# Normalised rows turned by a DMA transpose instead of TensorE, attention rows read from PSUM, and GpSimd's slot in another order

## The chip, the cores and the metric

The kernel runs on one core of a Trainium2 chip. A core has TensorE (PE, with its weight loads listed as PEld), VectorE (DVE), ScalarE (ACT), GpSimd (POOL) and SyncE (SP), which here only issues DMAs. Each engine works through its own list of instructions in order and waits on semaphores. The metric is the device time of one execution in microseconds; lower is better.

## The reference

The input holds 128 graphs of 128 nodes with 256 features each. The first step is a layernorm with ReLU; then come three layers, each an attention over the graph's neighbours and a feed-forward block of width 1024; at the end the input is added back.

```
h = max(layernorm(x), 0)
for l in 0..2:
    si, sj = h @ attn_w[l, :256], h @ attn_w[l, 256:]
    scores = leaky_relu(si[:, :, None] + sj[:, None, :] + attn_b[l], 0.2)
    attn   = softmax(where(adj + eye > 0, scores, -inf))
    n      = layernorm(h + attn @ h) * g1[l] + beta1[l]
    ff     = gelu(n @ W1[l] + b1[l]) @ W2[l] + b2[l]
    h      = layernorm(n + ff) * g2[l] + beta2[l]
return x + h
```

Everything is float32. The kernel computes each large product as three float16 products (high by high, high by low, low by high), where a value's low part is the value less its high part.

## The kernel before

Four graphs (`T` = 4) make one group, and one group in one layer is an item: 32 groups by 3 layers are 96 items. Items run in rings of eight groups: eight groups through layer 0, the same eight through layer 1, then layer 2, then the next eight. The program of every engine is a list of slots, one slot per item, written by hand: slot `s` holds the hidden layer of item `s`, and beside it the steps of neighbouring items: the end of item `s-1` and the attention of items `s+1` and `s+2`. Within a slot the order follows `c`, one of the eight blocks of 128 hidden columns.

TensorE's slot: for each `c` six matmuls of 512 columns for the hidden block (`hidden`, L366), then twelve of 256 columns for the feed-forward output (`feed`, L380), three blocks behind (`LAG` = 3), so that the first three blocks of a slot finish item `s-1`. After `c` = 0 the aggregation of item `s+1` (`aggregate`, L422: twelve matmuls). After `c` = 4 the eight transposes of item `s+1`'s normalised rows (`transpose_norm1`, L432) and the four of `spread_sj` for item `s+2` (L404), which spread a column of scores over the partitions. In `c` = 7 the four transposes of item `s+2`'s attention probabilities (`transpose_probs`, L410).

The normalised rows of item `s+1` are made like this. VectorE adds the aggregation to the rows (`attention_residual`, L650), takes their statistics (L579) and, after `hidden` of `c` = 0 in the next slot, aggregates them (L584 to L587). GpSimd raises the variance to the power -1/2 (L786) and forms the shift (L788). ScalarE applies both (`norm_attention`, L488, writing `norm1`). TensorE turns `norm1` into a PSUM bank pair (L432), ScalarE copies that to float16 `hT_hi` (`high_hT`, L534) and VectorE subtracts to get `hT_lo` (`split_hT`, L665). Both are needed by the first hidden block of the next slot: the first four matmuls read `hT_hi`, the last two `hT_lo`.

GpSimd's slot: `inverse_deviation` for item `s+1` (L786, L788); `h_residual`, two operations of 1024 elements (L798, L800), which waits until VectorE has made the dot products of item `s+2`; `low_X` (L804); then for item `s-1` `inverse_deviation`, `norm_feed` (L812, four operations) and, at the slot's end, `layer_output` (L826, L828, each twice). In slots whose item `s-2` is in layer 2 there is also `skip_connection` (L835), and in slots that start a group's layer 0 one more `inverse_deviation`.

VectorE's slot starts with the dot products of item `s+2` at `c` = 1 (L613 and L616, four of each, both reading `X` and `attn_rows` from SBUF). Of each hidden block, ScalarE makes the gelu (L478) and its float16 copy `g_hi` (L483), and VectorE the low part `g_lo` (L572); three PSUM banks hold hidden blocks (`PF_RING`), one bank the attention rows (`p_att`) and two pairs of banks (`p_pair`) the rest.

In the slots in which a new ring of groups comes in (eight of every 24, called heavy slots below; the others are light), VectorE takes the statistics of a group's input and makes its mask, and ScalarE makes the input's norm (`norm_input`, L488, four operations after `c` = 7).

All DMAs are issued by SP, in order, on one queue: group inputs `x_in` and `adj_in`, weights, stores and a second load of `x` for the last addition.

## Time and profile before

| | |
|---|---|
| median of three runs | 2402.95 us (2402.5 to 2403.74) |
| the profiled execution | 2401.22 us, span 2399.4 us |
| TensorE busy | 2333.0 us (97%) |
| ScalarE busy | 1892.0 us |
| VectorE busy | 1869.7 us |
| GpSimd busy | 1698.2 us |
| granted TensorE clock | 9 tenths or more in 39 of the page's 40 slices |
| DMA | 70.83 MB, 30 GB/s on average |

The profiled execution's span is what the trace covers; its own time is 1.8 us more. A matmul's duration in the trace is that of its whole passage through a pipelined array, so successive matmuls overlap, and the distance between their starts is what each costs.

### The profile page before, as it was taken

Reading aid. Unit: us, or ns where it says so; the run is one execution under the profiler, and the core shown is the slowest. Engines: PE = TensorE matmul, PEld = TensorE weight load, DVE = VectorE, ACT = ScalarE, POOL = GpSimd, SP = SyncE. Lnnn points to the kernel's source line nnn. Section 1 sums busy time; section 2 is a strip of 40 time slices with the busy share of each in tenths; the row PEclk is TensorE's granted clock in tenths of the full one; section 3 lists DMA queues with packets and bytes.
Section 4 is the critical chain, followed back from the end, with each engine's and each line's share of the span. In section 5 each row is a group of like instructions: output and inputs, shape, how many; then the busy total and the mean of one; then the engine's idle time right before and its main releaser. Section 6 shows DMA issues by size and latency. Waiting matters only on the chain.

```text
span 2399.4 us, 47629 instructions
## 1 busy us (share of the span) xinstructions
PE 2333.0 (97%) x16608; PEld 1649.3 (69%) x16608; DVE 1869.7 (78%) x5974; ACT 1892.0 (79%) x3498; POOL 1698.2 (71%) x1543
## 2 busy tenths in 40 slices
PE   3999999999999999999999999999999999999997
PEld 2667777776666777777666777777766677777775
DVE  6887777777888777777888787878788877787874
ACT  4878787878888878787888877778788887878783
POOL 3567676768887666667887767676878776767686
PEclk9999999999999999999999999999999999999998
DMA  5200000001211000001121000000121100000012
GB/s 162 87 28 27 1 1 2 1 19 41 93 62 36 1 1 1 1 1 36 54 78 60 23 2 1 1 1 2 53 67 63 41 2 1 1 1 1 19 42 65
DMA packets 77421, 70.83 MB, mean 30 GB/s; under 512 B 7040, under 2 KB 75648, under 8 KB 77184
## 3 DMA queue, kind: packets, MB, share of 16 engines
q1 hardware_dynamic: 77184, 67.79, 9.1%
q8 instruction: 134, 2.20, 0.4%
q14 instruction: 103, 0.84, 0.1%
HBM read 51.01 MB, written 16.78 MB: 28 GB/s over the span
## 4 chain that ended last, share of the span: by engine, by line
PE 66%; POOL 16%; DVE 11%; ACT 3%; issue 2%; POOLq 0%; DVEq 0%
PE p_pair L380 29%; PE p_hid L366 28%; PE p_pair L422 4%; PE p_pair L432 2%; POOL rstd L786 2%; DVE dots L613 2%; DVE g_lo L572 2%; POOL w_f L835 2%; POOL h_res L798 2%; POOL h_res L800 2%; POOL norm L812 2%; DVE res L675 2%; POOL w_f L828 2%; POOL X_lo L804 2%; POOL w_f L826 2%
## 5 line engine op out<-in xcount | busy, mean ns | idle before, releaser
L380 PE MATMUL p_pair<-w_hi,g_hi 128*128 128x256 f16 x3072 | 837.6, 273 | 0.0
L380 PE MATMUL p_pair<-w_lo,g_hi 128*128 128x256 f16 x3072 | 837.6, 273 | 0.0
L380 PE MATMUL p_pair<-w_hi,g_lo 128*128 128x256 f16 x3072 | 837.5, 273 | 0.0
L572 DVE TENSOR_TENSOR g_lo<-p_hid,g_hi 128x512 f16<-128x512 f32 x768 | 528.6, 688 | 396.2 <-ACT g_hi L483 389.7
L478 ACT ACTIVATE p_hid<-p_hid,b_eff 128x512 f32<-128x512 f32 x768 | 504.5, 657 | 316.9 <-PE p_hid L366 315.7
L798 POOL TENSOR_TENSOR h_res<-norm,g_rows 128x1024 f32<-128x1024 f32 x96 | 227.7, 2372 | 384.0 <-DVE res L675 377.3
L483 ACT ACTIVATE g_hi<-p_hid 128x512 f16<-128x512 f32 x768 | 458.6, 597 | 24.4
L366 PE MATMUL p_hid<-hT_hi,w_hi 128*128 128x512 f16 x1536 | 458.2, 380 | 1.5 <-DVE g_lo L572 1.4
L366 PE MATMUL p_hid<-hT_hi,w_lo 128*128 128x512 f16 x1536 | 458.3, 380 | 0.0
L366 PE MATMUL p_hid<-hT_lo,w_hi 128*128 128x512 f16 x1536 | 457.9, 380 | 0.0
L786 POOL TENSOR_TENSOR rstd<-var_eps,minus_half 128x4 f32<-128x4 f32 x224 | 242.2, 1081 | 259.0 <-DVE minus_mean L587 253.7
L380 PEld LDWEIGHTS p_pair<-w_lo,g_hi 128*128 128x128 f16 x3072 | 300.7, 98 | 106.5 <-issue 0.3
L380 PEld LDWEIGHTS p_pair<-w_hi,g_hi 128*128 128x128 f16 x3072 | 300.7, 98 | 105.6 <-issue 0.4
L380 PEld LDWEIGHTS p_pair<-w_hi,g_lo 128*128 128x128 f16 x3072 | 300.7, 98 | 34.8
L488 ACT ACTIVATE norm<-res,shift,rstd 128x256 f32<-128x256 f32 x384 | 199.4, 590 | 97.6 <-POOL shift L788 97.6
L366 PEld LDWEIGHTS p_hid<-hT_hi,w_lo 128*128 128x128 f16 x1536 | 150.6, 98 | 182.2 <-issue 1.7
L366 PEld LDWEIGHTS p_hid<-hT_lo,w_hi 128*128 128x128 f16 x1536 | 150.6, 98 | 182.2 <-issue 1.7
L579 DVE BATCH_NORM_STATS2 bn<-res 128x6 f32<-128x256 f32 x768 | 269.5, 416 | 3.3
L800 POOL TENSOR_TENSOR h_res<-h_res,res_rows 128x1024 f32<-128x1024 f32 x96 | 227.0, 2364 | 7.5
L812 POOL TENSOR_SCALAR norm<-res,rstd,shift 128x256 f32<-128x256 f32 x384 | 207.5, 555 | 10.0
L650 DVE SCALAR_TENSOR_TENSOR res<-p_pair,row_inv,X 128x256 f32<-128x256 f32 x384 | 159.1, 477 | 67.6 <-PE p_pair L422 67.5
L804 POOL TENSOR_TENSOR X_lo<-X,X_hi 128x1024 f16<-128x1024 f32 x96 | 204.6, 2132 | 0.0
(68 smaller groups left out, 3658.5 us busy)
## 6 DMA issues: line engine op xcount, KB each, us to landing
x_in<-in_x SPq DMA_DIRECT2D x32, 512.0 KB, 4.1
w_f<-in_x SPq DMA_DIRECT2D x32, 512.0 KB, 5.8
out<-w_f SPq DMA_DIRECT2D x32, 512.0 KB, 4.2
adj_in<-in_adj SPq DMA_DIRECT2D x32, 256.0 KB, 4.5
w_f<-in_L_gnn_W SPq DMA_DIRECT2D x6, 1024.0 KB, 6.1
attn_rows<-in_L_gnn_attn_w SPq DMA_DIRECT2D x1, 768.0 KB, 5.9
g_rows<-in_L_gnn_g SPq DMA_DIRECT2D x2, 384.0 KB, 7.5
b_rows<-in_L_gnn_b SPq DMA_DIRECT2D x1, 384.0 KB, 6.7
```

The costliest lines, as they stand in the source:

```text
L366: mm = pe.matmul(p_hid[in_ring(s, c, PF_RING)][:], w[l][:, k, cols], h[i][:, k, :], start=(n == 0), stop=(n == 3 * KD - 1))
L380: mm = pe.matmul(ff_banks(s)[:, t, :], g[i][:, nodes], w[l][:, c, :], start=(c == 0 and t % 2 == 0 and n == 0), stop=(c == C - 1 and n == ...
L478: act.activation(p_hid[k][:], p_hid[k][:], ACT.Gelu, bias=b1_eff[:, l, c:c + 1], scale=1.0 / WSCALE).then_inc(gelu_ready, 1)
L483: act.activation(g_hi[i][:], p_hid[k][:], ACT.Copy).then_inc(g_hi_ready, 1)
L488: act.activation(dst[:, t, :], src[:, t, :], func, bias=shift[n][s % 2][:, t:t + 1], scale=rstd[n][s % 2][:, t:t + 1]).then_inc(done, 1)
L572: dve.tensor_tensor(g_lo[i][:], p_hid[k][:], g_hi[i][:], ALU.subtract).then_inc(g_lo_ready, 1)
L579: dve.bn_stats(bn[n][:, t, :], src[:, t, :]).then_inc(stat_steps[n], 1)
L786: pool.tensor_tensor(rstd[n][s % 2][:], var_eps[n][:], minus_half[:], ALU.pow).then_inc(rstd_ready[n], 1)
L798: pool.tensor_tensor(h_res[i][:], norm1[:], rows(g1_rows, l, T), ALU.mult).then_inc(h_res_steps, 1)
L800: pool.tensor_tensor(h_res[i][:], h_res[i][:], rows(res_rows, l, T), ALU.add).then_inc(h_res_steps, 1)
L804: pool.tensor_tensor(X_lo[:], X[s % RING][:], X_hi[:], ALU.subtract).then_inc(X_lo_ready, 1)
L812: pool.tensor_scalar(norm2[:, t, :], res2[:, t, :], rstd[2][s % 2][:, t:t + 1], shift[2][s % 2][:, t:t + 1], ALU.mult, ALU.add).then_inc(n ...
```

## The change

1. `transpose_norm1`, `high_hT` and `split_hT` are gone. ScalarE copies `norm1` from SBUF to float16 `h_hi` (`high_h`, at `c` = 3), GpSimd subtracts to get `h_lo` (`low_h`), and SP issues one DMA transpose for each of the two (`turn_h`), 128x1024 float16 from SBUF to SBUF, into `hT_hi` and `hT_lo`. Both go on SP's queue, the high part first. TensorE's first hidden block waits for their landing.
2. The bank `p_att` is given up. The spread scores and the turned probabilities use halves of a bank pair (`sj_bank`, `pT_bank`), and the free bank holds `p_rows`, the layer's two attention rows, copied there once per eight items. The dot products read one operand from SBUF and one from PSUM, and stand at `c` = 5 for item `s+3`, where they stood at `c` = 1 for item `s+2`. Neither GpSimd's `h_residual` nor a wait for `X` of item `s-2` is tied to them any more.
3. GpSimd's slot is now: `inverse_deviation` of `s+1`; `inverse_deviation`, `norm_feed` and `layer_output` of item `s-2` (they were of `s-1`); `low_h` of `s+1`; `low_X`; `h_residual` of `s+1`; the input's `inverse_deviation`; `skip_connection`.
4. The input's statistics, its norm and its load come one slot earlier, and the program starts one slot earlier (`FIRST_SLOT` = -5).

GpSimd's list in a slot of layer 0 or 1 before; `rstd1` and `shift1` belong to the attention's norm, `rstd2` and `shift2` to the feed-forward's, and `X5` is an item's output:

```order
L786 TENSOR_TENSOR rstd1_0<-var_eps1,minus_half 128x4
L788 TENSOR_TENSOR shift1_0<-minus_mean1,rstd1_0 128x4
L798 TENSOR_TENSOR h_res0<-norm1,g1_rows 128x1024
L800 TENSOR_TENSOR h_res0<-h_res0,res_rows 128x1024
L804 TENSOR_TENSOR X_lo<-X1,X_hi 128x1024
L786 TENSOR_TENSOR rstd2_0<-var_eps2,minus_half 128x4
L788 TENSOR_TENSOR shift2_0<-minus_mean2,rstd2_0 128x4
L812 TENSOR_SCALAR norm2<-res2,rstd2_0,shift2_0 128x256 x4
L826 TENSOR_TENSOR X6<-norm2,g2_rows 128x512
L828 TENSOR_TENSOR X6<-X6,beta2_rows 128x512
```

and the same slot now (L834 and L836 stand twice each, as L826 and L828 did):

```order
L790 TENSOR_TENSOR rstd1_0<-var_eps1,minus_half 128x4
L792 TENSOR_TENSOR shift1_0<-minus_mean1,rstd1_0 128x4
L790 TENSOR_TENSOR rstd2_1<-var_eps2,minus_half 128x4
L792 TENSOR_TENSOR shift2_1<-minus_mean2,rstd2_1 128x4
L820 TENSOR_SCALAR norm2<-res2,rstd2_1,shift2_1 128x256 x4
L834 TENSOR_TENSOR X5<-norm2,g2_rows 128x512
L836 TENSOR_TENSOR X5<-X5,beta2_rows 128x512
L808 TENSOR_TENSOR h_lo<-norm1,h_hi 128x1024
L812 TENSOR_TENSOR X_lo<-X1,X_hi 128x1024
L800 TENSOR_TENSOR h_res0<-norm1,g1_rows 128x1024
L802 TENSOR_TENSOR h_res0<-h_res0,res_rows 128x1024
```

Before, one block of 1024 elements after another follows the first two rows; now `norm2` and the output of an older item stand between the attention's `shift1` and the new `h_lo`, whose operand `h_hi` ScalarE makes meanwhile.

ScalarE's list from the second hidden block of a slot to the sixth, before; `g_hi2` is the copy of a hidden block:

```order
L478 ACTIVATE p_hid2<-p_hid2,b1_eff 128x512
L483 ACTIVATE g_hi2<-p_hid2 128x512
L488 ACTIVATE norm1<-res1,shift1_1,rstd1_1 128x256 x4
L478 ACTIVATE p_hid0<-p_hid0,b1_eff 128x512
L483 ACTIVATE g_hi3<-p_hid0 128x512
L527 ACTIVATE X_hi<-X6 128x1024
L478 ACTIVATE p_hid1<-p_hid1,b1_eff 128x512
L483 ACTIVATE g_hi4<-p_hid1 128x512
L534 ACTIVATE hT_hi1<-p_pair1 128x1024
L478 ACTIVATE p_hid2<-p_hid2,b1_eff 128x512
L483 ACTIVATE g_hi5<-p_hid2 128x512
```

and now:

```order
L487 ACTIVATE p_hid2<-p_hid2,b1_eff 128x512
L492 ACTIVATE g_hi2<-p_hid2 128x512
L497 ACTIVATE norm1<-res1,shift1_1,rstd1_1 128x256 x4
L487 ACTIVATE p_hid0<-p_hid0,b1_eff 128x512
L492 ACTIVATE g_hi3<-p_hid0 128x512
L542 ACTIVATE h_hi<-norm1 128x1024
L487 ACTIVATE p_hid1<-p_hid1,b1_eff 128x512
L492 ACTIVATE g_hi4<-p_hid1 128x512
L536 ACTIVATE X_hi<-X6 128x1024
L487 ACTIVATE p_hid2<-p_hid2,b1_eff 128x512
L492 ACTIVATE g_hi5<-p_hid2 128x512
```

The copy to `hT_hi`, which stood behind `X_hi` and one more hidden block, is gone, and the copy to `h_hi` stands one hidden block ahead of `X_hi`.

```diff
+        p_rows = ps("p_rows", [P, 2, D])
         p_pair = [ps(f"p_pair{i}", [P, T, D]) for i in range(2)]
...
+        def sj_bank(s):
+            return agg_banks(s)[:, 0:2, :].rearrange("p a (u n) -> p (a u) n", n=N)
+        def pT_bank(s):
+            return agg_banks(s)[:, 2:4, :].rearrange("p a (u n) -> p (a u) n", n=N)
...
+            def turn_h(r, s):
+                i = s % 2
+                if later(r, s, 2):
+                    sp.wait_ge(hid_psum, total(r, s - 2, C, C))
+                for h, hT, made, turned in ((h_hi, hT_hi, h_hi_ready, hT_hi_ready), (h_lo, hT_lo, h_lo_ready, hT_lo_ready)):
+                    sp.wait_ge(made, total(r, s, 1, 1))
+                    sp.dma_start_transpose(hT[i][:].rearrange("p t k n -> p (t k) n"),
+                                           h[:].rearrange("p t d -> p (t d)")).then_inc(turned, 16)
...
                 if c == 0:
-                    pe.wait_ge(hT_hi_ready, total(r, s, 1, 1))
+                    pe.wait_ge(hT_hi_ready, total(r, s, 16, 16))
...
                     if c == 0 and n == 2 * KD:
-                        pe.wait_ge(hT_lo_ready, total(r, s, 1, 1))
+                        pe.wait_ge(hT_lo_ready, total(r, s, 16, 16))
...
             def spread_sj(r, s):
                 pe.wait_ge(dots_ready, total(r, s, 8, 8))
-                if later(r, s):
-                    pe.wait_ge(pT_lo_ready, total(r, s - 1, 1, 1))
+                if later(r, s, 3):
+                    pe.wait_ge(res2_ready, total(r, s - 3, 2, 2))
...
-            def transpose_norm1(r, s):
...
-                    if c == 4 and is_item(r, s + 1):
-                        transpose_norm1(r, s + 1)
...
+            def high_h(r, s):
+                act.wait_ge(norm1_ready, total(r, s, 4, 4))
+                if later(r, s):
+                    act.wait_ge(hT_hi_ready, total(r, s - 1, 16, 16))
+                act.activation(h_hi[:], norm1[:], ACT.Copy).then_inc(h_hi_ready, 1)
...
+                if q == 0 and pair == 0:
+                    dve.tensor_copy(p_rows[:], attn_rows[:, l]).then_inc(rows_ready, 1)
+                    dve.wait_ge(rows_ready, rows_total(r, s))
...
-                    if c == 1 and is_item(r, s + 2):
-                        if is_item(r, s - 2):
-                            dve.wait_ge(x_steps, x_total(r, s - 2, 4))
-                        dot_products(r, s + 2, 0)
-                        dot_products(r, s + 2, 1)
...
+                    if c == 5 and is_item(r, s + 3):
+                        dot_products(r, s + 3, 0)
+                        dot_products(r, s + 3, 1)
...
             def h_residual(r, s):
                 pool.wait_ge(norm1_ready, total(r, s, 4, 4))
-                if is_item(r, s + 1):
-                    pool.wait_ge(dots_ready, total(r, s + 1, 8, 8))
...
+            def low_h(r, s):
+                pool.wait_ge(h_hi_ready, total(r, s, 1, 1))
+                if later(r, s):
+                    pool.wait_ge(hT_lo_ready, total(r, s - 1, 16, 16))
+                pool.tensor_tensor(h_lo[:], norm1[:], h_hi[:], ALU.subtract).then_inc(h_lo_ready, 1)
...
                 if is_item(r, s + 1):
                     inverse_deviation(s + 1, 1, total(r, s + 1, 10, 10), total(r, s + 1, 2, 1))
-                    h_residual(r, s + 1)
+                if is_item(r, s - 2):
+                    inverse_deviation(s - 2, 2, total(r, s - 2, 10, 10), total(r, s - 2, 2, 1))
+                    norm_feed(r, s - 2)
+                    layer_output(r, s - 2)
+                if is_item(r, s + 1):
+                    low_h(r, s + 1)
                 if is_item(r, s + 2):
                     low_X(r, s + 2)
-                if is_item(r, s - 1):
-                    inverse_deviation(s - 1, 2, total(r, s - 1, 10, 10), total(r, s - 1, 2, 1))
-                    norm_feed(r, s - 1)
+                if is_item(r, s + 1):
+                    h_residual(r, s + 1)
```

## Rows read from the trace of the kernel before

**Rows 1.** The page's first part, TensorE, and its chain by engine:

```profile
PE 2333.0 (97%) x16608; PEld 1649.3 (69%) x16608; DVE 1869.7 (78%) x5974; ACT 1892.0 (79%) x3498; POOL 1698.2 (71%) x1543
...
PE 66%; POOL 16%; DVE 11%; ACT 3%; issue 2%; POOLq 0%; DVEq 0%
```

**Rows 2.** GpSimd's L798, once per slot: count, durations, first and last start:

```profile
L798 POOL TENSOR_TENSOR h_res<-norm,g_rows x96: 2351/2360/3176, 45.4 to 2346.7; 128x1024 f32<-128x1024 f32 x96
```

**Rows 3.** Timeline (start us, us, engine, line), TensorE in a light slot:

```profile
1516.26 0.59 PE L366 MATMUL p_hid<-hT_hi,w_hi 128*128 128x512 f16 x2
...
1517.12 0.59 PE L366 MATMUL p_hid<-hT_lo,w_hi 128*128 128x512 f16 x2
...
1518.87 0.27 PE L422 MATMUL p_pair<-X_hi,pT_hi 128*128 128x256 f16 x1
...
1520.07 0.27 PE L422 MATMUL p_pair<-X_hi,pT_lo 128*128 128x256 f16 x1
...
1530.60 1.04 PE L432 MATMUL p_pair<-ident,norm 128*128 128x128 f32 x8
...
1531.47 0.60 PE L404 MATMUL p_att<-ident,s_j 128*128 128x128 f32 x4
...
1531.91 0.59 PE L366 MATMUL p_hid<-hT_hi,w_hi 128*128 128x512 f16 x2
...
1538.41 0.60 PE L410 MATMUL p_att<-ident,probs 128*128 128x128 f32 x4
...
1540.16 0.59 PE L366 MATMUL p_hid<-hT_hi,w_hi 128*128 128x512 f16 x2
```

**Rows 4.** Timeline, TensorE's transposes in a heavy slot:

```profile
1216.00 1.09 PE L432 MATMUL p_pair<-ident,norm 128*128 128x128 f32 x8 [0.26 <-DVE res L675]
...
1224.11 0.66 PE L410 MATMUL p_att<-ident,probs 128*128 128x128 f32 x4
```

**Rows 5.** Timeline, VectorE between aggregation and statistics, light slot:

```profile
1520.38 1.66 DVE L650 SCALAR_TENSOR_TENSOR res<-p_pair,row_inv,X 128x256 f32<-128x256 f32 x4 [1.01 <-PE p_pair L422]
...
1524.61 0.15 DVE L587 TENSOR_REDUCE minus_mean<-mv 128x4 f32<-128x4 f32 x1
```

**Rows 6.** Timeline, GpSimd in the light slots:

```profile
1511.17 2.13 POOL L804 TENSOR_TENSOR X_lo<-X,X_hi 128x1024 f16<-128x1024 f32 x1
...
1513.26 1.03 POOL L786 TENSOR_TENSOR rstd<-var_eps,minus_half 128x4 f32<-128x4 f32 x1
...
1514.67 2.16 POOL L812 TENSOR_SCALAR norm<-res,rstd,shift 128x256 f32<-128x256 f32 x4
...
1516.80 1.26 POOL L826 TENSOR_TENSOR X<-norm,g_rows 128x512 f32<-128x512 f32 x1
...
1520.72 1.27 POOL L828 TENSOR_TENSOR X<-X,beta_rows 128x512 f32<-128x512 f32 x1
...
1524.83 1.02 POOL L786 TENSOR_TENSOR rstd<-var_eps,minus_half 128x4 f32<-128x4 f32 x1 [2.84 <-DVE minus_mean L587]
```

**Rows 7.** Timeline, ScalarE from the attention's norm on, light slot:

```profile
1526.18 2.08 ACT L488 ACTIVATE norm<-res,shift,rstd 128x256 f32<-128x256 f32 x4 [0.61 <-POOL shift L788]
...
1528.16 0.63 ACT L478 ACTIVATE p_hid<-p_hid,b_eff 128x512 f32<-128x512 f32 x1
...
1529.32 1.05 ACT L527 ACTIVATE X_hi<-X 128x1024 f16<-128x1024 f32 x1
```

**Rows 8.** DMA queues and issues: queue, packets, MB, share; size, issue to landing:

```profile
q1 hardware_dynamic: 77184, 67.79, 9.1%
...
x_in<-in_x SPq DMA_DIRECT2D x32, 512.0 KB, 4.1
...
adj_in<-in_adj SPq DMA_DIRECT2D x32, 256.0 KB, 4.5
```

**Rows 9.** DMA queues in the window 8 to 10 us, small packets alone:

```profile
DMA packets 2521, 0.02 MB, mean 8 GB/s; under 512 B 2520, under 2 KB 2520, under 8 KB 2521
...
q1 hardware_dynamic: 2521, 0.02, 75.4%
```

**Rows 10.** Waits by engine and line: total us, times, longest:

```profile
DVE g_lo L572 <- ACT g_hi L483: 389.7, 177, 4.1
...
POOL h_res L798 <- DVE res L675: 377.3, 93, 4.2
...
POOL rstd L786 <- DVE minus_mean L587: 253.7, 85, 12.3
...
PEld p_att L410 <- ACT probs L513: 42.0, 95, 4.8
```

**Rows 11.** Groups by line: count, busy us, mean ns, idle before:

```profile
L804 POOL TENSOR_TENSOR X_lo<-X,X_hi 128x1024 f16<-128x1024 f32 x96 | 204.6, 2132 | 0.0
...
L665 DVE TENSOR_TENSOR hT_lo<-p_pair,hT_hi 128x1024 f16<-128x1024 f32 x96 | 116.6, 1215 | 0.9 <-ACT hT_hi L534 0.9
...
L534 ACT ACTIVATE hT_hi<-p_pair 128x1024 f16<-128x1024 f32 x96 | 98.1, 1022 | 9.9 <-PE p_pair L432 2.2
```

**Rows 12.** Timeline, GpSimd's longer operations in a heavy slot:

```profile
1201.82 2.35 POOL L835 TENSOR_TENSOR w_f<-w_f 128x1024 f32<-128x1024 f32 x1
...
1216.12 2.36 POOL L798 TENSOR_TENSOR h_res<-norm,g_rows 128x1024 f32<-128x1024 f32 x1 [3.77 <-DVE res L675]
...
1218.56 2.36 POOL L800 TENSOR_TENSOR h_res<-h_res,res_rows 128x1024 f32<-128x1024 f32 x1
```

More of the change, by code:

```diff
@@ L192, in gnn_kernel @@
         h_res = [sb(f"h_res{i}", [P, T, D]) for i in range(2)]
-        hT_hi = [sb(f"hT_hi{i}", [P, KD, TN], F16) for i in range(2)]
-        hT_lo = [sb(f"hT_lo{i}", [P, KD, TN], F16) for i in range(2)]
+        h_hi, h_lo = sb("h_hi", [P, T, D], F16), sb("h_lo", [P, T, D], F16)
+        hT_hi = [sb(f"hT_hi{i}", [P, T, KD, N], F16) for i in range(2)]
+        hT_lo = [sb(f"hT_lo{i}", [P, T, KD, N], F16) for i in range(2)]
         g_hi = [sb(f"g_hi{i}", [P, TN], F16) for i in range(GS_RING)]
@@ L390, in fold_bias @@
                     for k in range(KD):
[L391 removed]
+                        mm = pe.matmul(bank[:, 0, c:c + 1], w1_f32[:, k, c * P:(c + 1) * P], beta1_col[:, l, k:k + 1],
                                        start=(k == 0), stop=(k == KD - 1))
@@ L700, in slot @@
             def slot(r, s):
-                starts = is_item(r, s + 4) and layer_of(s + 4) == 0
-                late = isinstance(r, int) and (r, s) == (0, -3)
-                if isinstance(r, int) and (r, s) == (0, -2):
+                starts = is_item(r, s + 5) and layer_of(s + 5) == 0
+                late = isinstance(r, int) and (r, s) == (0, -4)
+                if isinstance(r, int) and (r, s) == (0, -3):
                     dve.wait_ge(attn_dma, 2 * 16)
@@ L713, in slot @@
                         dve.wait_ge(stat_steps[2], total(r, s - 1, 10, 4))
-                    if c == 6 and starts and not late:
-                        dve.wait_ge(stat_steps[0], group_total(r, s + 4, 10, 4))
-                    if isinstance(r, int) and (r, s, c) == (0, -2, 3):
+                    if c == 2 and starts and not late:
+                        dve.wait_ge(stat_steps[0], group_total(r, s + 5, 10, 4))
+                    if isinstance(r, int) and (r, s, c) == (0, -3, 1):
                         dve.wait_ge(stat_steps[0], group_total(0, 1, 10, 4))
```

104 lines of the change are left out of this document (44 added, 60 removed).

## The prediction

> **What bounds the kernel now.** I read four views, in this order: the page's busy shares and chain, TensorE's timeline over one slot, the waits by line, and the timelines of GpSimd and VectorE over the same slot. TensorE is busy 97% of the span and two thirds of the chain run through it [rows 1]. GpSimd's first h_residual operation stands once in each of the 96 slots; from its first start, 45.4 us, to its last, 2346.7 us, are 95 slots, so a slot takes 24.22 us [rows 2]. A light slot takes 1540.16 - 1516.26 = 23.90 us, and within it every matmul starts as soon as the one before lets it; the norm's transposes take 1531.47 - 1530.60 = 0.87 us of that, those of the scores 0.44 us [rows 3]. In a heavy slot there is also a hole of 0.26 us or a little more ahead of the norm's transposes, for a bank pair that VectorE has not read yet [rows 4]. So TensorE sets the pace, and the other engines wait: VectorE 389.7 us for ScalarE, GpSimd 377.3 us before its h_residual and 253.7 us for the attention's statistics [rows 10].
>
> **What TensorE saves.** Eight transposes less per slot are 0.87 us, the hole in the heavy slots some 0.3 us in a third of the slots, together about 1.0 us. The hole goes because VectorE no longer makes the dot products ahead of the feed-forward residual, so that the residual ends earlier by their length; the wait is still there (it now guards the spread scores), with that cover, and costs the old 0.3 us if it is gone. What is late next on TensorE is the turned probabilities: their loads waited 42.0 us in 95 slots already [rows 10], and ScalarE's exponentials would come only as much earlier as the spread scores do. I put 0.2 us per slot back. If TensorE stays the bound, a slot takes 24.22 - 1.0 + 0.2 = 23.4 us.
>
> **What the other engines gain and lose, at nothing while covered.** VectorE loses the 1.22 us subtraction into hT_lo; ScalarE's copy of 1.02 us is replaced by one from SBUF, priced like X_hi, 1.05 us [rows 7, 11]. GpSimd gains low_h, which has the shape of low_X: 2.13 us per slot [rows 11]. Its fullest slot would hold three inverse deviations of 1.41, the norm 2.13, the output 5.2, low_h and low_X 2.13 each, h_residual 2 x 2.36 and the skip connection 2.35 us: 22.9 us [rows 6, 11, 12], just inside 23.4. The copy of the attention rows to PSUM, once per eight slots, I bound by 0 and 0.7 us (a VectorE operation of 512 elements), which is nothing. The dot products get a PSUM operand; the trace has them only with two SBUF operands, and the nearest PSUM row is the attention residual at 1.66 us for four [rows 5]: 0 to 0.1 us each, in a place (after the sixth hidden block) where VectorE waited.
>
> **The new chain.** The moved steps form a loop that closes once per slot, and I follow it through the light slot that begins at 1516.26 us. TensorE's first read of hT_lo is at 1517.12. Then come the rest of that block, a feed-forward block and the aggregation, whose last matmul starts at 1520.07; VectorE's residual starts at 1520.38, its last statistics operation at 1524.61, and GpSimd takes them up at 1524.83 [rows 3, 5, 6]. That is 7.71 us from the read of hT_lo. None of it moves. Before, GpSimd's two small operations were all that was needed: ScalarE applied the norm and TensorE turned it. Now GpSimd goes on in its new order:
> - the attention's and the feed-forward's inverse deviation, each 1514.67 - 1513.26 = 1.41 us: 2.82 us;
> - norm_feed, 1516.80 - 1514.67 = 2.13 us;
> - layer_output, 1516.80 to 1520.72 + 1.27: 5.19 us;
> - low_h, 2.13 us [rows 6, 11].
>
> So h_lo is made 7.71 + 2.82 + 2.13 + 5.19 + 2.13 = 19.98 us after the read of hT_lo. Its operand h_hi is no later: ScalarE ends the norm and one hidden block at 1529.32 and would end the copy at 1530.4, that is 13.3 us after that read, where GpSimd gets to low_h after 17.9 [rows 7]. Then the DMA transpose must land before TensorE's next read of hT_lo. With D for the time from SP's issue to the landing, the loop takes 20.0 + D. A slot cannot be shorter. All slots have it, light and heavy, and when it binds, GpSimd, VectorE and ScalarE have more room than before, so nothing else comes on top. It costs nothing only up to D = 3.4 us; the change as a whole is even at D = 4.2 us. Queued behind h_lo's transpose on SP is nothing that anyone waits for soon: the next loads and stores are a slot or more ahead. Ahead of it stands h_hi's transpose, issued some 6.7 us earlier, which is out of the way while D is below that.
>
> **How long is D.** The trace has no DMA transpose and no transfer from SBUF to SBUF, so I bound it by rows. The nearest in bytes is adj_in, 256 KB as here: 4.5 us from issue to landing [rows 8]. The queue's 77184 packets took 9.1% of 16 engines' 2399.4 us, 45 ns each, or 0.84 us for a 16th of 256 KB by bytes (67.79 MB in 3493 engine-us) [rows 8]. Adj_in's rows are 512 bytes, 32 packets per engine, 1.45 us at that mean, which leaves 3.05 us that are no transfer. The transpose reads 128 x 8 pieces of 256 bytes, 64 per engine.
> - By bytes: 3.05 + 0.84 = 3.9 us, the lower end.
> - By packets: 3.05 + 64 x 0.045 = 5.9 us.
> - In a stretch with only small packets, 2521 took 75.4% of 16 engines for 2 us, 9.6 ns each [rows 9]. If the turned rows are written in pieces of 16 elements (my guess for a small piece), 512 per engine, that is 3.05 + 4.9 = 8.0 us, the upper end.
>
> I take 4.9 us, between the first two, which is also nearest to adj_in's own 4.5. Then the slot takes 24.9 us.
>
> The Trainium skill has two prices for it. "Advanced Engine Details and Errata", section X-Bar Transpose (TRN2), says that transposing DMAs are as fast as plain ones; by that rule D would be adj_in's 4.5 us and the sum 2431 us. "VectorE: DVE Perf Modes", section The three transpose paths, gives 1309 ns for a 128x128 block through the DMA crossbar; eight in a row would be 10.5 us (an estimate from that page), and the sum far above my range. No row here shows either.
>
> **The sum.** The slots: 95 x (24.9 - 24.22) = +65 us. The start has its first hidden block behind one norm turned by DMA where TensorE and ScalarE did it; there ScalarE's probabilities were waited for anyway, so I add 2 us for it. 2399.4 + 65 + 2 = 2466 us of span, against the profiled execution's span; its own time was 1.8 us more, and the median of the runs another 1.7, so 2470 us.
>
> **Rivals.**
> - TensorE stays the bound (D at most 3.4 us, a transfer inside SBUF that lands sooner than any of the trace): 2399.4 + 95 x (23.4 - 24.22) + 2 + 3.5 = 2327 us. For it: the 3.05 us hold the way to and from HBM, which this transfer does not take, and x_in's twice as many bytes land in 4.1 us [rows 8]. Against it: even then 0.84 us of transfer leave 2.6 us for all else. Chance 0.13.
> - The loop binds a little, D from 3.4 to 4.2 us: faster by up to 75 us; at the lower end, 3.9 us, 2399.4 + 95 x (23.9 - 24.22) + 5.5 = 2375 us. Chance 0.17. Within 0.2% of before, D within 0.05 us of 4.2: 0.04.
> - My forecast, D from 4.3 to 6.5 us: 2404.9 + 95 x 0.08 to 95 x 2.28, that is 2413 to 2621 us, slower than before. Chance 0.42.
> - The crossbar writes small pieces or works block after block: at D = 8.0 us the slot takes 28.0 us and the sum is 2399.4 + 95 x 3.78 + 5.5 = 2764 us. From 6.7 us on the low part also queues behind the high part, and the time grows faster. For it: it is the only step here of which no row shows the kind, and it moves 2-byte elements one by one across partitions. Chance 0.24, half of it above 2765. By the 1309 ns of the Trainium skill's page "VectorE: DVE Perf Modes", section The three transpose paths, eight blocks in a row would put the kernel above 3000 us, an estimate.
> - The change doesn't shorten TensorE's list after all, since the probabilities' transposes wait by as much as the norm's are gone: then a slot cannot be below 24.2 us and small D give no gain, about 2405 us. I count it inside the second case; the rows of the exponentials' wait, 0.44 us per slot at most, speak against it [rows 10].
>
> Faster by over 0.2% (about what a measurement of this kernel tells from no change) is 0.30, within it 0.04, slower 0.66. The range goes from the TensorE bound, 2330, to the upper end of D, 2765 us; the likeliest case alone has 2413 to 2621.
>
> **What would show it.** In the changed profile TensorE's wait for hT_lo's transpose at each slot's start should be the longest of its waits, 1.5 us per slot at D = 4.9, and its busy share should fall to about 94%; the DMA list should show the transposes' time to landing, and GpSimd's operation into h_lo should start right after layer_output's last, with ScalarE long done. TensorE at 97% or more, with transposes landing in under 3.5 us, would be the first rival; a wait for hT_hi as well, ahead of the block's first matmul, would be the fourth. The prediction is wrong in its mechanism if GpSimd's low_h is waited for by someone else, or if TensorE's holes lie at the turned probabilities.

## The result: slower by 3.5%

The changed kernel takes 2485.98 us (median of four runs, 2485.15 to 2486.11), the kernel before 2403.18 us beside it (2402.5 to 2403.74): a ratio of 1.0348, 95% interval 1.0335 to 1.0361. The forecast was 2470 us, the range 2330 to 2765. The number came out nearly right; its reason did not.

The page of the changed kernel, the same parts as in [rows 1], and its DMA issues, whose last column is us from issue to landing:

```profile
span 2484.0 us, 46306 instructions
PE 2278.5 (92%) x15840; PEld 1561.2 (63%) x15840; DVE 1787.6 (72%) x5890; ACT 1894.5 (76%) x3498; POOL 1886.6 (76%) x1639
...
DVE 36%; PE 24%; POOL 17%; ACT 13%; issue 8%; DMA 1%; SPq 0%; DVEq 0%; POOLq 0%; ACTq 0%
...
L808 POOL TENSOR_TENSOR h_lo<-norm,h_hi 128x1024 f16<-128x1024 f32 x96 | 205.5, 2140 | 11.9 <-ACT h_hi L542 11.9
...
adj_in<-in_adj SPq DMA_DIRECT2D x32, 256.0 KB, 4.0
...
hT_hi<-h_hi SPq DMA_TRANSPOSE x96, 3.1
hT_lo<-h_lo SPq DMA_TRANSPOSE x96, 3.1
```

TensorE has 54.5 us less to do than before and 92% instead of 97% of the span. The chain has changed hands: two thirds of it were TensorE's [rows 1], now VectorE has 36%, and DMA 1%. The transposes land after 3.1 us, where the forecast rested on 4.9. The issue of one of them on SP, and the DMA packets in the window 1521.9 to 1525.2 us around it, in which the 16 DMA engines are busy from 1523.15 to 1524.55 us:

```profile
1521.93 1.23 SPq L327 DMA_TRANSPOSE hT_lo<-h_lo  x1
```

```profile
DMA packets 1056, 0.26 MB, mean 79 GB/s; under 512 B 1056, under 2 KB 1056, under 8 KB 1056
```

Hardly anything waits for the transposes: 0.9 us of TensorE's matmuls in the whole run. The waits by line (engine, its line, what ended the wait: us in total, times, longest us), against [rows 10]:

```profile
POOL rstd L790 <- DVE minus_mean L595: 509.3, 100, 14.2
...
DVE res L682 <- POOL norm L820: 294.4, 92, 3.6
DVE g_lo L580 <- ACT g_hi L492: 259.3, 242, 5.2
...
PE p_pair L431 <- ACT probs L522: 114.0, 94, 11.7
...
PE p_pair L425 <- DVE res L682: 41.1, 91, 0.6
```

The second line is the new one (before, no wait for the norm stands at this residual, L675): in 92 of 96 slots VectorE's feed-forward residual (`feed_residual`, L682) waits, for 3.2 us on average, for GpSimd's normalised rows. TensorE's own holes are the 114.0 us at the turned probabilities (L431) and 41.1 us at the spread scores (L425). Its wait for the low part's transpose, which the forecast priced at 1.5 us per slot, is 0.6 us in the whole run.

**The loop that binds.** The chain of waits over one light slot (start, us, what; TensorE, VectorE, ScalarE and GpSimd hand one thread around):

```profile
1502.74 1.31 PE p_pair L401 x12
1504.06 1.32 PE p_pair L443 x12
...
1505.40 1.67 DVE res L661 x4
...
1509.71 0.08 DVE minus_mean L595
...
1509.86 1.03 POOL rstd L790
...
1511.15 0.96 POOL rstd L790
...
1512.50 2.17 POOL norm L820 x4
...
1514.80 1.29 DVE res L682 x2
1516.09 0.52 DVE g_lo L580
1516.61 1.40 DVE bn L587 x4
...
1518.64 1.13 DVE scores L642 x4
...
1519.79 0.70 DVE row_top L648
...
1520.51 0.03 ACT minus_max L516
...
1522.85 1.35 ACT probs L522 x7
...
1524.25 0.66 PE p_pair L431 x4
1524.91 1.31 PE p_pair L401 x12
```

Read it as a ring. There is one buffer `res2`. VectorE may write group s-1's feed-forward residual into it only when GpSimd's `norm_feed` has read group s-2's. In the new order `norm_feed(s-2)` stands behind `inverse_deviation(s+1)`, which waits for VectorE's attention statistics (L595). Before, `norm_feed` of that item was made one slot sooner, at the end of the slot before (in [rows 6] at 1514.67 us, 1.6 us ahead of TensorE's slot; now at 1512.50 us, 11.2 us behind the slot's start at 1501.29), so the same wait never held. Now the residual starts when the norm ends; behind it in VectorE's order stand the statistics, the scores and their maxima (TensorE's spread scores wait for the residual too, but are done at 1516.85 us, ahead of VectorE's scores at 1518.64); then come ScalarE's exponentials, TensorE's turned probabilities, and behind those on TensorE a feed-forward block, the next slot's first hidden block, another feed-forward block and the aggregation; from that come the attention residual and its statistics, and GpSimd's first step again. By the rows: VectorE from the attention residual to the statistics 4.4 us, GpSimd 4.8, VectorE again 5.7, ScalarE 3.7, and TensorE from its probabilities (1524.25) to the next attention residual (1505.40 + 24.77 = 1530.17) 5.9; with the gaps 24.8 us. From one of GpSimd's starts into `X_lo` to the next are 24.77 us in light slots and 25.30 in heavy ones (23.90 and 24.67 before). TensorE is busy for 23.42 us of such a slot.

**The three parts of the 84.6 us.** The first kind of matmul of the hidden blocks, count, durations and first and last start, of the kernel before and of the changed one:

```profile
L366 PE MATMUL p_hid<-hT_hi,w_hi x1536: 376/379/634, 51.9 to 2376.1; 128*128 128x512 f16 x192
```

```profile
L387 PE MATMUL p_hid<-hT_hi,w_hi x1536: 376/379/635, 60.4 to 2463.5; 128*128 128x512 f16 x192
```

The start is 8.5 us later; from the first to the last is 2403.1 us instead of 2324.2, so the slots cost 78.9; what is left behind it is 2.8 us shorter (20.5 instead of 23.3).

The start has one cause that a row shows (e11 tests it), VectorE's third input statistics (first column its start, in brackets its idle time and what ended it):

```profile
22.49 1.41 DVE L587 BATCH_NORM_STATS2 bn<-x_in 128x6 f32<-128x256 f32 x4 [7.46 <-DMA x_in<-in_x]
```

The dot products of group 0, which everything behind them needs, stand after this operation now; they are done at 28.3 us, where the kernel before had them at 18.9.

### The profile page after: what moved, and what is told of

Its sections match the earlier page's. It is cut to its first block, busy times and chain, and to the rows that moved or that the text cites. A ratio compares the mean times of both kernels' runs of the same rounds, so it can differ in the third digit from the quotient of the medians.

```text
span 2484.0 us, 46306 instructions
## 1 busy us (share of the span) xinstructions
PE 2278.5 (92%) x15840; PEld 1561.2 (63%) x15840; DVE 1787.6 (72%) x5890; ACT 1894.5 (76%) x3498; POOL 1886.6 (76%) x1639
## 4 chain that ended last, share of the span: by engine, by line
DVE 36%; PE 24%; POOL 17%; ACT 13%; issue 8%; DMA 1%; SPq 0%; DVEq 0%; POOLq 0%; ACTq 0%
PE p_pair L401 10%; DVE bn L587 10%; POOL norm L820 8%; POOL rstd L790 7%; DVE res L661 6%; PE p_hid L387 6%; ACT probs L522 5%; ACT L522 5%; PE p_pair L443 5%; DVE res L682 5%; DVE g_lo L580 5%; DVE scores L642 4%; DVE row_top L648 3%; PE p_pair L431 2%; ACT leaky L517 2%
## 5 line engine op out<-in xcount | busy, mean ns | idle before, releaser
L682 DVE SCALAR_TENSOR_TENSOR res<-p_pair,h_res 128x512 f32<-128x512 f32 x192 | 123.6, 686 | 297.7 <-POOL norm L820 294.4
L808 POOL TENSOR_TENSOR h_lo<-norm,h_hi 128x1024 f16<-128x1024 f32 x96 | 205.5, 2140 | 11.9 <-ACT h_hi L542 11.9
```

Source lines behind the costliest of these rows:

```text
L682: dve.scalar_tensor_tensor(out=res2[:, pair, :], in0=ff_banks(s)[:, pair, :], scalar=1.0 / WSCALE, in1=h_res[s % 2][:, pair, :], op0=ALU.m ...
```

## The experiments

Theory A, formed from the trace above: the ring through `res2`, 24.8 us, is the bound, and it comes from GpSimd's order alone. Rival B (the one on record): the ring through GpSimd's `low_h` and the landing of its transpose. Rival C: the transposes' DMA traffic slows the core by itself. All ratios are to the kernel before, timed beside each; it took 2401.7 to 2403.3 us. Slot times are distances between GpSimd's starts into `X_lo`, one per slot.

| kernel | us | ratio, 95% interval | light slot | heavy slot |
|---|---|---|---|---|
| before | 2403.18 | 1 | 23.90 | 24.67 |
| changed | 2485.98 | 1.0348 (1.0335 to 1.0361) | 24.77 | 25.30 |
| e1, two `res2` | 2379.67 | 0.9906 (0.9892 to 0.9921) | 23.39 | 24.86 |
| e2, norm first | 2369.42 | 0.9862 (0.9847 to 0.9876) | 23.38 | 24.90 |
| e3, low part first | 3186.69 | 1.3266 (1.3244 to 1.3288) | 32.4 (mean of all) | |
| e4, order alone | 2533.44 | 1.0545 (1.053 to 1.0561) | 25.44 | 25.75 |
| e6, skip moved | 2341.15 | 0.975 (0.9734 to 0.9766) | 23.38 | 23.38 |
| e7, dots from SBUF | 2577.95 | 1.0738 (1.0722 to 1.0754) | 25.0, some 25.4 | 27.1 to 28.6 |
| e8, order back | 2388.77 | 0.9947 (0.9932 to 0.9961) | 23.39 | 24.1 to 25.1 |
| e10, low part last | 2884.48 | 1.2013 (1.1992 to 1.2034) | 29.3 (mean of all) | |
| e11, dots first | 2334.68 | 0.9714 (0.97 to 0.9729) | 23.38 | 23.38 |
| e12, skip moved, two `res2` | 2341.9 | 0.9744 (0.9728 to 0.9761) | 23.38 | 23.38 |

### e1: a second residual buffer

The changed kernel with one thing of theory A's ring cut. For the room, the scratch of the dot products has seven pieces instead of eight; VectorE has two more waits, one for the piece used twice and one for GpSimd's inverse deviation of item s-2.

```diff
-        res2 = sb("res2", [P, T, D])
+        res2 = [sb(f"res2_{i}", [P, T, D]) for i in range(2)]
...
-                if later(r, s):
-                    dve.wait_ge(norm2_ready, total(r, s - 1, 4, 4))
+                if later(r, s, 2):
+                    dve.wait_ge(norm2_ready, total(r, s - 2, 4, 4))
```

> The changed kernel with two buffers for the feed-forward residual res2, so that VectorE writes item s-1's while GpSimd still reads item s-2's; one scratch piece of the dot products is reused to make room. Theory A (the slot is a loop: GpSimd's norm_feed of item s-2 lets VectorE write res2, that lets TensorE spread the scores, then scores, exponentials, turned probabilities, aggregation, statistics, GpSimd again): the loop opens, a slot falls from 24.8 to about 23.4 us, 2484 us of span to about 2335; TensorE's holes before the spread scores and before the probabilities shrink from 0.6 and 1.0 us to under 0.3. Theory B (the loop on record, GpSimd's low_h and the landing of hT_lo): low_h and the DMA are where they were, 2484 us. Theory C (the DMA traffic slows the core): 2484 us.

2379.67 us, 106 less than the changed kernel. The light slots fell to 23.39 us, TensorE's own work; the residual's wait for the norm is gone. The recorded ring is untouched by this edit, and would have left the time where it was. The span of 2377.6 us is 43 above A's figure; 35 of that are in the 24 heavy slots, 1.47 us each above the light ones, see e6.

### e2: the norm first

The same cut from the other side: no new buffer, but `norm_feed(s-2)` ahead of `inverse_deviation(s+1)` on GpSimd, so that it doesn't stand behind VectorE's statistics.

```diff
+                if is_item(r, s - 2):
+                    inverse_deviation(s - 2, 2, total(r, s - 2, 10, 10), total(r, s - 2, 2, 1))
+                    norm_feed(r, s - 2)
                 if is_item(r, s + 1):
                     inverse_deviation(s + 1, 1, total(r, s + 1, 10, 10), total(r, s + 1, 2, 1))
                 if is_item(r, s - 2):
...
-                    inverse_deviation(s - 2, 2, total(r, s - 2, 10, 10), total(r, s - 2, 2, 1))
-                    norm_feed(r, s - 2)
                     layer_output(r, s - 2)
```

> The changed kernel with GpSimd's inverse deviation and norm_feed of item s-2 moved ahead of the attention's inverse deviation, one res2 buffer as before; layer_output stays behind. Theory A: norm_feed ends some 7 us earlier in its idle time, the loop opens, 23.4 us in light slots and some tenths more where the skip connection fills GpSimd, 2335 to 2350 us. Theory B: low_h comes 3.5 us earlier, the loop through hT_lo is 3.5 us shorter and TensorE is the bound: 2330 us as well, so this run does not part A from B, only both from C, which says 2484 us.

2369.42 us, light slots 23.38. Two different edits that both break ring A give the same light slot. This one shortens the recorded ring as well, so it is e1 that parts the two. The time lies 19 us above the expected range: 18 heavy slots took 24.90 us, 1.5 us each above the light ones, see e6.

### e3: the low part first

`low_h` directly behind `inverse_deviation(s+1)`, ahead of the feed-forward's norm. This takes 8.7 us (norm, output and an inverse deviation) out of the recorded ring and puts `low_h` and its wait for ScalarE into A's.

```diff
                     inverse_deviation(s + 1, 1, total(r, s + 1, 10, 10), total(r, s + 1, 2, 1))
+                if is_item(r, s + 1):
+                    low_h(r, s + 1)
                 if is_item(r, s - 2):
...
-                if is_item(r, s + 1):
-                    low_h(r, s + 1)
```

> The changed kernel with low_h right behind the attention's inverse deviation on GpSimd, ahead of the feed-forward's inverse deviation and norm_feed. Theory A: GpSimd waits for h_hi, which ScalarE ends 5.4 us after GpSimd's start, then 2.1 us of low_h, so norm_feed ends 6.3 us later and each slot takes that much more: about 31 us, 3080 us in all. Theory B: hT_lo lands some 5 us earlier, the time falls to the TensorE bound, 2330 us. Theory C: 2484 us.

3186.69 us: the sign and nearly the size of A's forecast, 857 us away from the rival's. Waits by line:

```profile
DVE res L682 <- POOL norm L820: 893.6, 93, 10.0
...
PE p_pair L425 <- DVE res L682: 636.0, 91, 7.9
POOL h_lo L808 <- ACT h_hi L542: 411.6, 96, 4.3
```

The low part waits 4.3 us in each slot for ScalarE's copy, and norm and residual stand behind it. The 107 us above A's figure, 1.4 us per slot against its 31 us, go with a mean granted TensorE clock of 0.872: in one slot TensorE stands still for 6.9 us until 1513.55 us, and then works for 3.6 us at a granted clock of 0.50, which costs it 1.8 us. How much of the 107 us that is was not taken apart.

### e4: GpSimd's order alone

The kernel before with nothing but GpSimd's new order (and without the one VectorE wait that this order fulfils by itself).

```diff
                     inverse_deviation(s + 1, 1, total(r, s + 1, 10, 10), total(r, s + 1, 2, 1))
-                    h_residual(r, s + 1)
+                if is_item(r, s - 2):
+                    inverse_deviation(s - 2, 2, total(r, s - 2, 10, 10), total(r, s - 2, 2, 1))
+                    norm_feed(r, s - 2)
+                    layer_output(r, s - 2)
...
-                if is_item(r, s - 1):
-                    inverse_deviation(s - 1, 2, total(r, s - 1, 10, 10), total(r, s - 1, 2, 1))
-                    norm_feed(r, s - 1)
+                if is_item(r, s + 1):
+                    h_residual(r, s + 1)
...
-                if is_item(r, s - 1) and not (isinstance(r, int) and PER * r + s == ITEMS):
-                    layer_output(r, s - 1)
```

> The kernel before, with TensorE's transposes of the normalised rows and no DMA transpose, and only GpSimd's slot turned as in the change: the feed-forward's inverse deviation, norm_feed and layer_output for item s-2 behind the attention's inverse deviation, then low_X, then h_residual; VectorE's wait for item s-2's output ahead of the dot products is left out, which ordered nothing that is read. Theory A: the loop is the same without any DMA, 24.8 us in light and 25.3 in heavy slots against 23.9 and 24.7: 2399 plus about 76, 2475 us. Theories B and C: no DMA, no loss, 2400 us.

2533.44 us, with no DMA transpose in the kernel: the order alone costs more than the whole change. It is 58 us above A's figure, because the ring's GpSimd part is longer here. From the chain of waits (the same columns as above):

```profile
1511.20 1.21 POOL rstd L784
...
1512.81 2.56 POOL norm L810 x4
...
1515.50 1.29 DVE res L675 x2
```

The norm takes 2.56 us instead of 2.17 and the inverse deviation 1.21 instead of 0.96. In this kernel VectorE's dot products, both operands in SBUF, run from 1510.32 to 1513.4 us, beside them. The two differences are 0.64 us of the 0.67 us by which this ring's light slot exceeds the changed kernel's.

### e6: the skip connection moved

In e2 the heavy slots still took 24.90 us. VectorE makes the mask there. e2, VectorE and then GpSimd in one heavy slot:

```profile
1220.01 2.61 DVE L608 CUSTOM_DVE_ANT_0 adj_in<-eye_i,adj_in 128x1024 uint16<-128x1024 uint16 x1
...
1223.60 1.65 DVE L661 SCALAR_TENSOR_TENSOR res<-p_pair,row_inv,X 128x256 f32<-128x256 f32 x4
```

```profile
1219.72 2.35 POOL L843 TENSOR_TENSOR w_f<-w_f 128x1024 f32<-128x1024 f32 x1
1222.03 1.47 POOL L790 TENSOR_TENSOR rstd<-var_eps,minus_half 128x4 f32<-128x4 f32 x1
```

GpSimd's `skip_connection` (L843) started first; the mask's addition, two SBUF operands, beside it took 2.61 us, and the attention residual behind it is on the way to the next norm. e6 is e2 with the skip connection one slot later, right behind `norm_feed`.

```diff
                     norm_feed(r, s - 2)
+                if is_item(r, s - 3) and layer_of(s - 3) == L - 1:
+                    skip_connection(r, s - 3)
...
-                if is_item(r, s - 2) and layer_of(s - 2) == L - 1:
-                    skip_connection(r, s - 2)
```

> e2_norm_first with GpSimd's skip connection moved from the slot's end to behind norm_feed in the next slot. In e2's heavy slots (24.9 us against 23.4 in light ones) VectorE's mask operation, whose two operands both lie in SBUF, takes 2.60 us where it starts beside the skip connection's 2.35 us operation, against 0.66 to 0.78 us elsewhere, and it stands on the chain. Theory P (the two engines shut each other out for an operation): the mask operation falls to 0.7 to 1.1 us and the heavy slots to 23.1 to 23.7 us: 18 of them (three rings of six) give back some 1.3 us each, 2369 to about 2345 us. Theory Q (heavy slots are bound by ScalarE, which has the input's norm there): nothing, 2369 us.

2341.15 us, every slot 23.38. The edit also takes the skip connection out of GpSimd's work ahead of the norm in the heavy slots, but GpSimd had 2.0 us to spare there in e2 (its idle time ahead of the attention's inverse deviation). The same operation in a heavy slot of e6:

```profile
1204.60 0.66 DVE L608 CUSTOM_DVE_ANT_0 adj_in<-eye_i,adj_in 128x1024 uint16<-128x1024 uint16 x1
```

### e7: the dot products from SBUF

e2 with the dot products reading the attention rows from SBUF again; the copy to PSUM stays.

```diff
-                    dve.tensor_tensor_reduce(out=dots[:, 2 * t, :], in0=X[q][:, t, :], in1=p_rows[:, 0, :], scale=1.0,
+                    dve.tensor_tensor_reduce(out=dots[:, 2 * t, :], in0=X[q][:, t, :], in1=attn_rows[:, l, 0, :], scale=1.0,
...
-                    dve.tensor_tensor_reduce(out=dots[:, 2 * t + 1, :], in0=X[q][:, t, :], in1=p_rows[:, 1, :], scale=1.0,
+                    dve.tensor_tensor_reduce(out=dots[:, 2 * t + 1, :], in0=X[q][:, t, :], in1=attn_rows[:, l, 1, :], scale=1.0,
```

> e2_norm_first with the dot products reading the attention rows from SBUF again; the copy to PSUM stays in, unread. They run beside GpSimd's h_residual, two operations of 2.36 us with two SBUF operands. Theory P (VectorE's operations with two SBUF operands and GpSimd's shut each other out): the dot products, 3.0 us for eight in e2, take 3 to 5 us more, or h_residual grows by as much; VectorE has 2.2 us of idle time behind them, so a slot costs 0.5 to 2.5 us more: 2410 to 2600 us. Theory Q (no such thing, PSUM makes no difference): 2369 us.

2577.95 us, 209 us more than e2. VectorE and GpSimd of e7 in one slot:

```profile
1505.73 2.56 DVE L627 CUSTOM_DVE_ANT_0 dots<-X,attn_rows 128x256 bf16<-128x256 f32 x1
...
1508.22 2.56 DVE L624 CUSTOM_DVE_ANT_0 dots<-X,attn_rows,attn_b_col 128x256 bf16<-128x256 f32 x1
...
1510.71 0.41 DVE L627 CUSTOM_DVE_ANT_0 dots<-X,attn_rows 128x256 bf16<-128x256 f32 x1
```

```profile
1505.47 2.54 POOL L800 TENSOR_TENSOR h_res<-norm,g_rows 128x1024 f32<-128x1024 f32 x1
1508.09 2.41 POOL L802 TENSOR_TENSOR h_res<-h_res,res_rows 128x1024 f32<-128x1024 f32 x1
```

One dot product of 0.4 us falls beside each of GpSimd's two operations, and each takes 2.56 us and ends 0.3 us behind it. The mean over the run is 1058 ns where the changed kernel has 474. With an operand in PSUM none of this happens, though there too dot products run beside `h_residual`. So in this order of GpSimd's steps the second part of the change is worth 209 us; the kernel before kept the two apart by making `h_residual` wait for the dot products.

### e8: GpSimd's order put back

The changed kernel with the DMA transposes and the PSUM rows, and GpSimd in the order of before (`low_h` behind `h_residual`).

```diff
-                if is_item(r, s - 2):
-                    inverse_deviation(s - 2, 2, total(r, s - 2, 10, 10), total(r, s - 2, 2, 1))
-                    norm_feed(r, s - 2)
-                    layer_output(r, s - 2)
+                if is_item(r, s + 1):
+                    h_residual(r, s + 1)
...
+                if is_item(r, s - 1):
+                    inverse_deviation(s - 1, 2, total(r, s - 1, 10, 10), total(r, s - 1, 2, 1))
+                    norm_feed(r, s - 1)
...
+                if is_item(r, s - 1) and not (isinstance(r, int) and PER * r + s == ITEMS):
+                    layer_output(r, s - 1)
```

> The changed kernel with GpSimd's order turned back: attention's inverse deviation, h_residual, then the new low_h, low_X, then inverse deviation and norm_feed of item s-1, skip connection, the input's inverse deviation, layer_output of s-1. The DMA transposes, the PSUM rows and the moved dot products stay. Theory A (the loss is the turned order alone): norm_feed of an item ends in the slot before it is waited for, light slots take 23.4 us, 2335 to 2375 us in all. A rival (the DMA transposes or the shared banks cost something themselves): 2400 us or more.

2388.77 us, 0.5% less than before and 14 us above A's range, with light slots of 23.39 us. Together with e4 this settles the cause: the order without the transposes loses, the transposes without the order gain. The heavy slots stay at 24.1 to 25.1 us; the mask's addition takes 1438 ns on average here against 708 in e6, so the cause of e6 is in them too; that it is the whole of it was not tried.

### e10: the low part last

The recorded ring made longer: e2 with `low_h` behind `low_X` and `h_residual`.

```diff
-                if is_item(r, s + 1):
-                    low_h(r, s + 1)
...
                     h_residual(r, s + 1)
+                if is_item(r, s + 1):
+                    low_h(r, s + 1)
```

> e2_norm_first with low_h behind low_X and h_residual, 6.9 us later. This tests the loop on record, which in the changed kernel had room, with its landing of 3.1 us instead of 4.9: 7.71 from the read of hT_lo to GpSimd's start, 1.25 inverse deviation, 5.16 output, 2.13 low_X, 4.76 h_residual, 2.13 low_h, 3.1 to the landing, some 0.1 for semaphores: 26.2 us per slot, that is 2369 plus 95 x (26.2 - 23.8) = about 2600 us, with TensorE waiting for the DMA. If the landing is no part of a loop or takes longer beside TensorE's reads, 2369 us or well above 2620.

2884.48 us; the light slots take 28.8 and 29.2 us in turn, 29.0 on average, where 26.2 were expected. The ring of the forecast exists, then, and now it binds: in 94 slots TensorE waits for the landing, 382.0 us in all. One such wait, and the 4 us behind it (behind the window and its length stand the busy times of PE, PEld, DVE, ACT and POOL, and behind those the granted clock, 0.50):

```profile
1512.70 1.03 PE L387 MATMUL p_hid<-hT_lo,w_hi 128*128 128x512 f16 x2 [4.00 <-DMA hT_lo<-h_lo]
```

```profile
1512.70:1516.70 4.00, 4.00 (x17) 2.56 (x18) 0.00 (x0) 1.26 (x2) 3.82 (x7) 0.50 0.83 270
```

The chain of waits of e10 at the same place, and in a later light slot:

```profile
1509.58 3.07 DMA hT_lo<-h_lo
...
1513.73 2.56 PE p_pair L401 x12
1516.29 2.46 PE p_pair L443 x12
```

```profile
1717.21 1.04 PE p_hid L387 x2
1718.25 2.17 PE p_pair L401 x12
1720.41 1.32 PE p_pair L443 x12
```

TensorE has stood still for 4.0 us, and about then its granted clock falls to one half: 1.2 instead of 2.4 GHz. In the first of these slots, a heavy one in which inputs and an output are moved too, it is at half from about 1511.7 to 1518.5 us, 6.8 us; in the light slots it is at half for some 3.4 us (1716.5 to 1719.9 in this one). TensorE's part of the ring, from its read of `hT_lo` to VectorE's residual, lies just there: 6.1 us in the first slot, 4.6 and 4.9 in turn in light ones, against 3.25 at full clock in the changed kernel (1502.15 to 1505.40). The landing is still 3.1 us. So two things that the expectation had left out stand on the ring: `low_X` waits 1.2 us or more per slot for ScalarE, and TensorE takes 1.5 us longer. The expectation's own terms add up to 26.3, not 26.2; with these two they come to 29.0 us, the mean of the light slots.

### e11: the dot products first in the start

e6 with the third group's input statistics behind the first dot products, in the start alone.

```diff
-                late = isinstance(r, int) and (r, s) == (0, -4)
+                late = isinstance(r, int) and (r, s) in ((0, -4), (0, -3))
...
                         dot_products(r, s + 3, 1)
+                    if c == 5 and isinstance(r, int) and (r, s) == (0, -3):
+                        input_statistics(0, 2)
+                        dve.wait_ge(stat_steps[0], group_total(0, 2, 10, 4))
+                        aggregates(0, group_total(0, 2, 10, 8))
```

> e6_skip_moved (2341.15 us against 2401.2 of the kernel before in its own comparison) with one thing turned in the very first slot of VectorE: the dot products of group 0 ahead of the statistics of the third group. In the changed kernel VectorE sits from 15.0 to 22.5 us for the third x_in there (7.46 us idle) with group 0's first dot products behind it, while the kernel before had made them by 18.9 us; its first hidden block starts at 51.9 us, that of the changed kernel at 60.4, that of e6_skip_moved at 61.3. Theory S (the late start is this one wait): s_j is ready near 19 to 20 us, the fold of the bias starts there instead of at 29.1, and the first hidden block comes near 52 to 53 us; with slots of 23.38 us behind it the whole falls by 8 to 9 us, to about 2332. Rival T (the start is set by the loads of weights and masks, or by the changed slots' longer reach): the first hidden block stays at 58 to 61 us and the time within 2 us of 2341.

2334.68 us, the fastest kernel of this study, 2.9% below the kernel before. The first hidden block starts at 53.0 us instead of 61.3 (the first start in this row):

```profile
L387 PE MATMUL p_hid<-hT_hi,w_hi x1536: 376/379/634, 53.0 to 2311.8; 128*128 128x512 f16 x192
```

The start is 8.3 us shorter; from the first hidden block to the last are 2258.8 us against 2257.4 in e6. The whole is 6.5 us shorter than e6, and 7.2 us shorter than e12, which was timed beside it; the expectation had 8 to 9.

### e12: both cures

e6 with e1's two residual buffers as well; its edits are the two shown above.

> e6_skip_moved with two buffers for the feed residual beside it (and one piece less of scratch for the dot products, for the room). The light and the heavy slots of e6_skip_moved last 23.38 us, TensorE's own work. Theory A (after norm_feed went first the wait of VectorE's feed residual for the normalised rows of the group before sets nothing any more, and TensorE's work bounds every slot): a second buffer brings nothing, 2339 to 2344 us, slots 23.38 us. Rival B (the residual buffer still costs in some slots): below 2337 us.

2341.9 us, the same as e6. With the norm first and the skip connection moved, the second buffer buys nothing.

## Why the prediction was right in its number and wrong in its reason

- **TensorE's savings: right.** "A slot takes 24.22 - 1.0 + 0.2 = 23.4 us" if TensorE stays the bound. Wherever nothing else binds (e1, e2, e6, e8, e11, e12) the light slot is 23.38 or 23.39 us.
- **The prices of the added steps: right.** `low_h` 2.14 us (forecast 2.13), the copy to PSUM 0.68 us at the upper bound given, a dot product with a PSUM operand 474 ns against 482 before. That this operand also keeps the dot products out of GpSimd's way, worth 209 us in e7, was not in the forecast at all.
- **The ring through `low_h`: its length right, its place wrong.** "19.98 us after the read of hT_lo": TensorE reads it at 1502.15, GpSimd ends h_lo at 1519.78 + 2.13 = 1521.91, 19.76 us. With the landing the ring is 22.9 us long, below TensorE's 23.4, so it held nothing up; e10 shows it binding when made longer.
- **The size of D: wrong.** 4.9 us was taken and 3.1 measured, below even the lower end of 3.9. The step that failed is the 3.05 us "that are no transfer", worked out from adj_in, a load from HBM, and carried over to a transfer within SBUF. Of the transpose's 3.1 us 1.4 are transfer and 1.7 are not, 1.23 of them the issue. The forecast had 3.05 and, at its 4.9 us, 1.85. Its 64 pieces per engine were nearly right (1056 packets are 66), but each cost 21 ns and not 45. With D right, the forecast's own rule gives 2327 us, the first rival, which had a chance of 0.13. Its condition came true and its time did not.
- **"When it binds, GpSimd, VectorE and ScalarE have more room than before, so nothing else comes on top": the step that failed most.** The forecast priced `norm_feed` (2.13 us) as a thing that stands ahead of `low_h`, and did not ask who waits for it. The waiter is in the code: `feed_residual` waits for `norm2_ready` of the item before. The change moves that item's norm 12.8 us later, about half a slot, and behind a wait for VectorE. Without this ring the slots would have been shorter by 1.4 us light (e2 against the changed kernel), and 116.6 us in all.
- **What is late next: the right place, a wrong size and no cause.** "The turned probabilities", at 0.2 us per slot: measured 1.2 us (114.0 in 94 slots), because the scores stand behind the late residual in VectorE's order. The hole that was to go, at the residual, came back as the wait of the spread scores, 41.1 us in 91 slots. The forecast named holes at the probabilities as what would make its mechanism wrong, and they did.
- **The start: 2 us forecast, 8.5 measured.** Only the way to the first transposed rows was weighed; the dot products, one slot ahead, had been put behind a load on VectorE. e11 takes most of it back.
- **GpSimd "22.9 us, just inside 23.4": right as a sum, and not enough.** It has room, but in heavy slots its skip connection fell beside VectorE's mask and stretched it from 0.66 to 2.6 us in e1 and e2 (in the changed kernel itself the two mostly miss each other: 755 ns on average). e6 without that is at TensorE's bound in all slots.

So two errors met: a loop priced 1.5 us per slot too dear (24.9 against the bound of 23.4) and a loop overlooked that lies 1.4 us above TensorE's bound in a light slot and 1.9 in a heavy one. The agreement within 16 us is an accident.

## What to carry to other kernels

When a step moves in one engine's order, list for each thing that the step *frees* or produces who waits for it, above all with single buffers, and follow that waiter around until it comes back to the step: a ring that closes once per iteration sets the pace when it is longer than the busiest engine's work, however idle every engine on it looks. A table of busy shares can't show this: all engines but TensorE had a quarter of the span free here. And an engine's own order can be cured more cheaply than with a buffer: the norm, which others waited for, ahead of a step that itself waits (e2), did as much in the light slots as a second buffer (e1), and beside it the buffer adds nothing (e12).

## What the runs showed of the hardware

- A DMA transpose of 128x1024 float16 within SBUF lands 3.1 us after its issue begins: 1.23 us of issue on SP, 1.4 us of transfer at 184 GB/s, and 0.5 us behind that. The load of adj_in, as many bytes from HBM, takes 4.0 us in the same run. The Trainium skill, "Advanced Engine Details and Errata", section X-Bar Transpose (TRN2), says that transposing DMAs are as fast as plain ones; here the transpose is no slower than that load, but no run has a plain transfer within SBUF to compare. The Trainium skill, "VectorE: DVE Perf Modes", section The three transpose paths, has 1309 ns for a block of 128x128; eight blocks in 3.1 us show that this price doesn't add up over the blocks of one transfer.
- VectorE and GpSimd get in each other's way when VectorE reads two operands from SBUF. VectorE was held until GpSimd's operation ended: a dot product took 2.56 us instead of 0.42 beside `h_residual` (e7), the mask's addition 2.61 instead of 0.66 beside the skip connection (e2), while a dot product with one operand in PSUM kept its 474 ns. Beside the norm in e4 it was GpSimd that paid: 2.56 us instead of 2.17, while the dot products kept their 0.42 to 0.48 us. The Trainium skill, "SBUF — State Buffer", section Who interferes with whom, says the same in its own terms: a VectorE instruction with two SBUF inputs contends with a GpSimd instruction that reads SBUF, and one with at most one SBUF input does not. Trace and page agree.
- TensorE's granted clock fell to 0.50 around the end of a stretch of 4.0 us without work, and stayed there for 3.4 us in light slots and 6.8 us in the heavy slot shown (e10). The changed kernel's holes, 1.2 and 0.4 us per slot, left it at 0.994 over the run. So a wait of 4.0 us on TensorE in each slot cost the wait and 1.3 to 1.7 us more behind it in light slots.
